# Block scales of the feed-forward tiles: five of their six small operations moved from VectorE to GpSimd

## Chip, cores, metric

One Trainium2 chip, one core of it. The metric is the device time of one execution in microseconds, the median of several runs.

## What is computed

A small vision tower: patches to tokens, an RWKV attention layer, a feed-forward layer with quantized operands, a softmax attention layer, and a mixture of 64 experts. 64 images of 17 tokens make 1088 rows of 256 numbers. The change lies in the feed-forward layer, whose hidden values (1024 for each row) are quantized to a 4-bit format in blocks of 16 before the down projection:

```
def fake_quant_nvfp4(x, global_scale):
    xb = x.reshape(sh[:-1] + (sh[-1] // BLOCK, BLOCK))
    amax = jnp.max(jnp.abs(xb), axis=-1, keepdims=True)
    sc = jnp.clip(amax / FP4_MAX * global_scale, 0.0, FP8_MAX)
    sc8 = sc.astype(jnp.float8_e4m3fn).astype(jnp.float32)
    dq = sc8 / global_scale
    safe_dq = jnp.where(dq == 0.0, 1.0, dq)
    a = jnp.clip(jnp.abs(xb) / safe_dq, 0.0, FP4_MAX)
    q = jnp.sign(xb) * _FP4_VALS[jnp.digitize(a, _FP4_MIDS)]
    return (q * dq).reshape(sh)
gate_out = nvfp4_linear(x, gate_w, s_in[0])
up_out = nvfp4_linear(x, up_w, s_in[0])
hidden = jax.nn.silu(gate_out) * up_out
return nvfp4_linear(hidden, down_w, s_in_down[0])
```

A row has 64 blocks, so a tile of 128 rows has 128 x 64 block scales, and each is made from the block's maximum by a chain of six operations.

## The kernel before

Every engine has its program written out by hand; semaphores are the only order between them. The feed-forward layer goes over 9 tiles of 128 rows (the last has 64). For tile n:

- TensorE makes gate and up products into PSUM (`gate_up`), ScalarE makes silu of the gate (L1312), and VectorE multiplies both into `hid` (L1710).
- VectorE takes the maxima of the 64 blocks into `ham` (L1718), and makes the scales in six small operations on 128 x 64 elements: scaled and clipped maximum `a0` (L1729), its lower bound `low` (L1732), `low` times a power of two plus `a0` (L1738, which rounds to 8 bits), the rounded scale with its sign turned, twice over, in `hsb` (L1744), its product with the inverse of the global scale (L1752), and the reciprocal (L1754). `hss` holds three such rows and there are two of them.
- GpSimd multiplies `hid` by the reciprocals (L623, the division), ScalarE makes its absolute value as 16-bit numbers in `hq` (L1295).
- Two tiles later VectorE rounds it in four large operations of 128 x 1024: L1724, L1735, L1741 (a clamp), and L1749 (times the scale in `hsb`). TensorE transposes `hq`, ScalarE moves it, TensorE makes the down product, and VectorE adds it to `h` (L1468) four tiles after n.

VectorE's loop (L1700 on) has in its pass n the small operations of tile n and the rounding of tile n-2, one in the gaps of the other: while a small operation waits for the one before, a large one is issued. `mark` and `after` count them on one semaphore, `link` is both at once. GpSimd has nothing in this stage but the division, and two memsets before the division of tile 5 (L619, L620), which clear parts of `qT` and `kbd` for the attention. Where the last tile is done, layernorm and attention follow.

Two other places come up below, both in the attention stage: `L644`, GpSimd's four copies of a block of `prT` into `pbd`, each waiting for the one before, and `L1812`, VectorE's subtraction of one SBUF tensor from another (`shared_w` less `shared_h`), twice without a wait between.

Of the kernel before, what the change touches and what calls it, by code (L numbers as in the profile page):

```python
# [15 lines left out]
ALU = mybir.AluOpType  # L16
ACT = mybir.ActivationFunctionType
AX = mybir.AxisListType
# [16 lines left out]
PAIRS = BLK // 2  # L35
E_MAGIC = 2.0 ** 20
Q_MAGIC = 2.0 ** 22
Q_FLOOR = Q_MAGIC * (1.0 + 2.0 ** -7)
# [20 lines left out]
def rows(t):  # L59
    return min(P, N - t * P)  # L60


def bc(ap, axis, n):

    a = ap.unsqueeze(axis)
    shape = list(a.shape)
    shape[axis] = n
    return a.broadcast_to(shape)
# [40 lines left out]
def build(nc, A, out):  # L109
    with ExitStack() as ctx:  # L110
        def sem(name):
            return ctx.enter_context(nc.semaphore(name))
# [24 lines left out]
        gs6 = sb("gs6", [P, 5])  # L137
        gin = sb("gin", [P, 5])
        gil = sb("gil", [P, 5])
# [64 lines left out]
        hid = [reg2.cut([P, I0]) for _ in range(3)]  # L204
        hq = [reg2.cut([P, I0], BF16) for _ in range(4)]
        hqT = [reg2.cut([P, IC, P], BF16) for _ in range(2)]
        ham = [reg2.cut([P, NHB]) for _ in range(2)]
        hss = [reg2.cut([P, 3, NHB]) for _ in range(2)]
        hsm = [reg2.cut([P, NHB], BF16) for _ in range(2)]
        hsb = [reg2.cut([P, 2 * NHB], BF16) for _ in range(3)]  # L210
# [141 lines left out]
        s_xdiv = sem("s_xdiv")  # L352
        s_xabs = sem("s_xabs")
        s_hdiv = sem("s_hdiv")
        s_hinv = sem("s_hinv")
        s_habs = sem("s_habs")
        s_y0 = sem("s_y0")
# [15 lines left out]
        s_hq = sem("s_hq")  # L373
# [193 lines left out]
        def _(pool):  # L567
# [29 lines left out]
            def largest(m):  # L597

                pool.wait_ge(s_wmx, m + 1)
                nc.gpsimd.partition_all_reduce(wmx_all[:, m:m + 1], wmx[:, m:m + 1], P, RMAX).then_inc(s_wmxa, 1)  # L600

            largest(0)
            largest(1)
            nc.gpsimd.memset(upto[:, :], 0.125).then_inc(s_mc, 1)
# [11 lines left out]
            for t in range(NT):  # L616
                if t == 5:
                    pool.wait_ge(s_xqT, 3)
                    nc.gpsimd.memset(qT[:, :, T:SLOT], 0.0).then_inc(s_zero, 1)  # L619
                    nc.gpsimd.memset(kbd, 0.0).then_inc(s_zero, 1)  # L620
                pool.wait_ge(s_hinv, t + 1)
                v = hid[t % 3].rearrange("p (k b r) -> p k b r", k=PAIRS, r=2)
                nc.gpsimd.tensor_tensor(v, v, bc(bc(hss[t % 2][:, 2, :], 1, PAIRS), 3, 2), ALU.mult).then_inc(s_hdiv, 1)  # L623
                if t == NT - 1:
                    ln(2, 0)
# [828 lines left out]
        def _(dve):  # L1454
            chain = [0]

            def link(ins):

                chain[0] += 1
                ins.then_inc(s_dve, 1)  # L1460
                dve.wait_ge(s_dve, chain[0])

            V = nc.vector
# [7 lines left out]
            def mark(ins):  # L1471

                chain[0] += 1
                ins.then_inc(s_dve, 1)
                return chain[0]

            def after(count):
                dve.wait_ge(s_dve, count)
# [94 lines left out]
            def round_weight(m):  # L1573
# [10 lines left out]
                                   op0=ALU.mult, op1=ALU.add).then_inc(s_clsb, 1)  # L1584
# [115 lines left out]
            for n in range(NT + 5):  # L1700
                if n == NT + 3:
                    low_part(0, 0)
                    low_part(1, 1)
                scales, rounding, adding = n < NT, 0 <= n - 2 < NT, 0 <= n - 4 < NT
                if scales:
                    am, (a0, a1, a2) = ham[n % 2], [hss[n % 2][:, i, :] for i in range(3)]
                    low, neg, v, r = hsm[n % 2], hsb[n % 3], hid[n % 3], slice(0, rows(n))
                    dve.wait_ge(s_gate, n + 1)
                    dve.wait_ge(s_gu, 2 * n + 2)
                    V.scalar_tensor_tensor(out=v[r, :], in0=ps[r, 4:6, :].rearrange("p a b -> p (a b)"), scalar=alp[r, 1:2],  # L1710
                                           in1=gate[n % 2][r, :], op0=ALU.mult, op1=ALU.mult).then_inc(s_hid, 1)
                if adding:
                    t = n - 4
                    dve.wait_ge(s_down, t + 1)
                    add_rows(t, 7 if t % 2 else 0, alp[0:rows(t), 2:3], s_h2)
                if scales:
                    dve.wait_ge(s_hid, n + 1)
                    done_s = mark(V.tensor_reduce(am, v.rearrange("p (k b r) -> p b k r", k=PAIRS, r=2), AX.XY, ALU.max,  # L1718
                                                  apply_absolute_value=True))
                if rounding:  # L1720
                    w = n - 2
                    x, q = hid[w % 3], hq[w % 4]
                    dve.wait_ge(s_habs, w + 1)
                    done_r = mark(V.scalar_tensor_tensor(out=x, in0=q, scalar=Q_FLOOR, in1=x, op0=ALU.max, op1=ALU.add))  # L1724
                if scales:
                    after(done_s)
                    if n >= 2:
                        dve.wait_ge(s_hdiv, n - 1)
                    done_s = mark(V.tensor_scalar(a0, am, gs6[:, 4:5], 448.0, ALU.mult, ALU.min))  # L1729
                if scales:  # L1730
                    after(done_s)
                    done_s = mark(V.tensor_scalar(low, a0, 2.0 ** -6, None, ALU.max))  # L1732
                if rounding:
                    after(done_r)
                    done_r = mark(V.scalar_tensor_tensor(out=q, in0=q, scalar=Q_FLOOR, in1=x, op0=ALU.max, op1=ALU.subtract))  # L1735
                if scales:
                    after(done_s)
                    done_s = mark(V.scalar_tensor_tensor(out=a1, in0=low, scalar=E_MAGIC, in1=a0, op0=ALU.mult, op1=ALU.add))  # L1738
                if rounding:
                    after(done_r)  # L1740
                    done_r = mark(V.tensor_scalar(q, q, 6.0, -6.0, ALU.min, ALU.max))  # L1741
                if scales:
                    after(done_s)
                    done_s = mark(V.scalar_tensor_tensor(out=neg.rearrange("p (b r) -> p b r", r=2), in0=bc(low, 2, 2),  # L1744
                                                         scalar=E_MAGIC, in1=bc(a1, 2, 2), op0=ALU.mult, op1=ALU.subtract))
                if rounding:
                    after(done_r)
                    q = q.rearrange("p (k c) -> p k c", k=PAIRS)
                    V.tensor_tensor(q, q, bc(hsb[w % 3], 1, PAIRS), ALU.mult).then_inc(s_hq, 1)  # L1749
                if scales:  # L1750
                    after(done_s)
                    done_s = mark(V.tensor_scalar(a2, neg[:, 0::2], gil[:, 4:5], 1e-24, ALU.mult, ALU.max))  # L1752
                    after(done_s)
                    V.reciprocal(a2, a2).then_inc(s_hinv, 1)  # L1754
                if n - 4 == LN_PARTS[0][1] - 1:
                    ln_variance(2, 0)
                if n - 4 == LN_PARTS[0][1]:
                    ln_finish(2, 0)
# [287 lines left out]
```

## Time and profile before

| | |
|---|---|
| median of 3 runs | 623.29 us (622.12 to 624.65) |
| the profiled execution | 625.0 us, its span 623.3 us |
| VectorE busy | 439.4 us (70%) |
| GpSimd busy | 218.7 us (35%) |
| TensorE busy | 518.0 us (83%) |
| feed-forward tiles, first L1710 to last L1754 | 126.90 to 188.31 us of the span |

The times of single operations, waits and the chain that ended last come from the one profiled execution. An operation's row in the timeline has its start, its duration, the engine and the line, output and inputs by name with their shapes, and in brackets how long the engine had been idle before it and who released it. Nearly all tiles of this stage lie in one large allocation called `region`, so rows are told apart by their lines.

### The profile page before, as it was taken

What the parts mean: (1) busy time and instruction counts of PE and PEld (TensorE: products, weight loads), DVE (VectorE), ACT (ScalarE), POOL (GpSimd) and SP (SyncE); (2) the same over time, 40 slices, a digit from 0 to 9 for tenths busy, and PEclk for the clock granted to TensorE, in tenths of its full rate; (3) what the DMA queues carried; (4) which work ended last, traced back from release to release, by engine and by line L of the source; (5) the groups of instructions that cost most, each with busy time, mean ns of one, the idle gap of its engine ahead of it and who ended that gap; (6) DMA issues with size and microseconds to landing.
All of it is one profiled execution on the core that took longest, in us unless ns stands there. A gap on an engine that the chain in (4) does not pass through costs nothing.

```text
span 623.3 us, 10367 instructions
## 1 busy us (share of the span) xinstructions
PE 518.0 (83%) x3494; PEld 421.2 (68%) x3498; DVE 439.4 (70%) x995; ACT 337.6 (54%) x798; POOL 218.7 (35%) x230
## 2 busy tenths in 40 slices
PE   3986953166555699999999999999999999999875
PEld 2755842023323699999999887876777777777674
DVE  4996998999999546555655713576776777775676
ACT  1577635255444656666666325625666677676600
POOL 2101001022422602222221141237777777777600
PEclk9985987586875699999999999999999999999979
DMA  8980000008200000000000001013777777887492
GB/s 270 381 315 0 1 0 0 0 2 272 79 2 0 1 26 27 26 28 27 26 1 2 2 1 51 22 28 100 200 225 203 230 237 216 230 241 212 143 407 87
DMA packets 43895, 67.33 MB, mean 108 GB/s; under 512 B 11022, under 2 KB 27015, under 8 KB 43716
## 3 DMA queue, kind: packets, MB, share of 16 engines
q1 hardware_dynamic: 36868, 64.62, 32.5%
q0 software_dynamic: 6976, 2.07, 1.7%
q8 instruction: 28, 0.46, 0.3%
q14 instruction: 23, 0.19, 0.1%
HBM read 66.81 MB, written 17.20 MB: 135 GB/s over the span
## 4 chain that ended last, share of the span: by engine, by line
PE 60%; DVE 24%; DMA 5%; ACT 4%; issue 3%; POOL 3%; SPq 0%; DVEq 0%; POOLq 0%; ACTq 0%
PE ps L1089 9%; PE ps L734 6%; PE ps L736 6%; PE ps L735 6%; PE ps L953 5%; PE ps L911 5%; PE ps L786 4%; PE ps L741 4%; DMA region<-x_rows,region 3%; PE ps L943 3%; PE ps L1079 2%; PE ps L925 2%; PE ps L1136 2%; DVE region L1724 2%; PE ps L1097 2%
## 5 line engine op out<-in xcount | busy, mean ns | idle before, releaser
L1089 PE MATMUL ps<-region 128*128 128x352 f32 x256 | 86.4, 460 | 0.3 <-issue 0.3
L1780 DVE TENSOR_TENSOR region<-ps,region 32x136 f32<-32x136 f32 x128 | 38.1, 298 | 55.3 <-PE ps L911 53.8
L685 POOL DMA_INDIRECT region<-x_rows,region x64 | 68.1, 1064 | 20.2 <-issue 15.0
L734 PE MATMUL ps<-nTh,high 128*128 128x272 f32 (+2 forms) x248 | 74.4, 300 | 0.4 <-ACT region L1362 0.4
L735 PE MATMUL ps<-nTl,high 128*128 128x272 f32 (+2 forms) x248 | 71.6, 289 | 0.0
L694 POOL DMA_INDIRECT y_rows<-region x60 | 61.1, 1019 | 21.0 <-issue 14.7
L644 POOL COPY region<-region 32x544 f32<-32x544 f32 x32 | 26.4, 825 | 115.1 <-DVE region L1799 113.6
L1928 DVE SCALAR_TENSOR_TENSOR region<-region,ps 128x176 f32<-128x176 f32 x64 | 25.4, 397 | 42.9 <-ACT region L1439 40.3
L736 PE MATMUL ps<-nTh,pairs_low 128*128 128x272 f32 x192 | 55.6, 290 | 0.0
L1449 ACT ACTIVATE high<-region 88x512 fp32r<-88x512 f32 x64 | 40.3, 630 | 25.4 <-PE ps L736 20.0
L1089 PEld LDWEIGHTS ps<-region 128*128 128x128 f32 x256 | 43.6, 190 | 14.0 <-issue 0.5
L734 PEld LDWEIGHTS ps<-nTh,high 128*128 128x128 f32 (+2 forms) x248 | 46.3, 187 | 2.0 <-ACT region L1362 0.6
L735 PEld LDWEIGHTS ps<-nTl,high 128*128 128x128 f32 (+2 forms) x248 | 46.4, 187 | 0.1
L595 POOL TENSOR_TENSOR rstd<-veps,mhalf 128x6 f32<-128x6 f32 (+1 forms) x8 | 9.2, 1148 | 100.6 <-DVE veps L1487 100.6
L734 PE MATMUL ps<-high,pairs_low 88*128 88x256 f32 x128 | 41.3, 323 | 3.0 <-DVE shared_low L1953 3.0
L623 POOL TENSOR_TENSOR region<-region 128x1024 f32<-128x1024 f32 x9 | 19.2, 2129 | 63.3 <-DVE region L1754 63.3
L741 PE MATMUL ps<-region 128*128 128x256 f32 (+1 forms) x108 | 28.6, 420 | 10.2 <-DMA region<-patches 10.2
L736 PEld LDWEIGHTS ps<-nTh,pairs_low 128*128 128x128 f32 x192 | 36.5, 190 | 0.0
L735 PE MATMUL ps<-w_low,pairs_low 88*128 88x256 f32 x128 | 36.1, 282 | 0.0
L736 PE MATMUL ps<-high,pairs_low 88*128 88x256 f32 x128 | 36.0, 281 | 0.0
L911 PE MATMUL ps<-region 128*128 128x136 f32 x256 | 33.1, 282 | 0.9 <-DVE region L1780 0.9
L953 PE MATMUL ps<-region 128*128 128x256 f32 (+1 forms) x144 | 31.8, 381 | 2.0 <-DVE region L1780 1.5
(264 smaller groups left out, 1353.4 us busy)
## 6 DMA issues: line engine op xcount, KB each, us to landing
region<-moe_w SPq DMA_DIRECT2D x64, 352.0 KB, 3.7
region<-moe_w SPq DMA_DIRECT2D x64, 176.0 KB
y_rows<-zrow SPq DMA_DIRECT2D x1, 6528.0 KB, 25.3
region<-y_rows SPq DMA_DIRECT2D x8, 768.0 KB, 10.5
region<-wqkv SPq DMA_DIRECT2D x8, 384.0 KB, 3.0
region<-ffn_w SPq DMA_DIRECT2D x2, 1024.0 KB, 8.3
region<-patches SPq DMA_DIRECT2D x3, 384.0 KB, 8.3
region<-patches SPq DMA_DIRECT2D x1, 1152.0 KB, 10.7
```

The source lines that it names most:

```text
L644: nc.gpsimd.tensor_copy(pbd[j][r, :, q * T:(q + 1) * T], prT[r, :, 0:T]).then_inc(s_spread, 1)
L685: nc.gpsimd.indirect_dma_start(out=xb[m8], out_offset=None, in_=x_rows, in_offset=bass.IndirectOffsetOnAxis(ap=sloti[:, at:at + 1], axis=0 ...
L694: nc.gpsimd.indirect_dma_start(out=y_rows, out_offset=bass.IndirectOffsetOnAxis(ap=sld[m8], axis=0), in_=yb[m], in_offset=None, bounds_che ...
L734: nc.tensor.matmul(out, parts_a[0], parts_b[0], start=first, stop=False)
L735: nc.tensor.matmul(out, parts_a[0], parts_b[1], start=False, stop=False)
L736: return nc.tensor.matmul(out, parts_a[1], parts_b[0], start=False, stop=last)
L741: nc.tensor.matmul(ps[0:rows(t), t % 8, 0:D], patch[:, c, t * P:t * P + rows(t)], tokw[:, c, :], start=(c == 0), stop=False)
L911: mm = nc.tensor.matmul(ps[:, 4 + g // 2, (g % 2) * 2 * GW:(g % 2 + 1) * 2 * GW], qT[:, 4 * t:4 * t + 4, :].rearrange("p b t -> p (b t)"), ...
L953: mm = nc.tensor.matmul(ps[0:rows(t), 4 + t % 4, 0:D], attnT[:, c, t * P:t * P + rows(t)], wo1[:, c, :], start=(c == 0), stop=(c == HP - 1))
L1089: mm = nc.tensor.matmul(ps[:, 2 + m % 2, 0:2 * EI], xbT[m % 2][:, c, :], w13[m][:, c, :], start=(c == 0), stop=(c == DC - 1))
L1449: nc.scalar.activation(w2_h[m % 2], w2[m], ACT.Copy).then_inc(s_w2h, 1)
L1780: last = V.tensor_tensor(sc[r, s0:s0 + 8, 0:T].rearrange("p (a b) t -> p a b t", a=4), ps[r, 4:8, 0:4 * GW].rearrange("p a (b h t) -> p a ...
```

## The change

The first five of the six small operations go to GpSimd, in front of its division of the same tile, each waiting for the one before on a semaphore of its own (`s_hsc`). VectorE keeps the maxima (which now signal `s_ham`) and the reciprocal, which it issues after the whole rounding of tile n-2. The rounding operations, which had the small ones between them, are linked directly. On GpSimd `low` is made as the lower bound times the power of two in one operation, so that the third and the fourth are plain operations on two tensors; it is kept in 32 bits. Two waits are new for the buffers: the maxima wait for the reciprocal two tiles before, and GpSimd's operation 4 and its division wait for the rounding (`s_hq`).

```diff
+            def tile_scales(t):
+                am, (a0, a1, a2) = ham[t % 2], [hss[t % 2][:, i, :] for i in range(3)]
+                low, neg = a2, hsb[t % 3]
+                pool.wait_ge(s_ham, t + 1)
+                nc.gpsimd.tensor_scalar(a0, am, gs6[:, 4:5], 448.0, ALU.mult, ALU.min).then_inc(s_hsc, 1)
+                pool.wait_ge(s_hsc, 5 * t + 1)
+                nc.gpsimd.tensor_scalar(low, a0, 2.0 ** -6, E_MAGIC, ALU.max, ALU.mult).then_inc(s_hsc, 1)
+                pool.wait_ge(s_hsc, 5 * t + 2)
+                nc.gpsimd.tensor_tensor(a1, low, a0, ALU.add).then_inc(s_hsc, 1)
+                pool.wait_ge(s_hsc, 5 * t + 3)
+                if t >= 3:
+                    pool.wait_ge(s_hq, t - 2)
+                nc.gpsimd.tensor_tensor(neg.rearrange("p (b r) -> p b r", r=2), bc(low, 2, 2), bc(a1, 2, 2),
+                                        ALU.subtract).then_inc(s_hsc, 1)
+                pool.wait_ge(s_hsc, 5 * t + 4)
+                nc.gpsimd.tensor_scalar(a2, neg[:, 0::2], gil[:, 4:5], 1e-24, ALU.mult, ALU.max).then_inc(s_hsc, 1)
+                pool.wait_ge(s_hinv, t + 1)
...
-                pool.wait_ge(s_hinv, t + 1)
+                tile_scales(t)
                 v = hid[t % 3].rearrange("p (k b r) -> p k b r", k=PAIRS, r=2)
+                if t >= 2:
+                    pool.wait_ge(s_hq, t - 1)
...
                 if scales:
                     dve.wait_ge(s_hid, n + 1)
-                    done_s = mark(V.tensor_reduce(am, v.rearrange("p (k b r) -> p b k r", k=PAIRS, r=2), AX.XY, ALU.max,
-                                                  apply_absolute_value=True))
+                    if n >= 2:
+                        dve.wait_ge(s_hinv, n - 1)
+                    V.tensor_reduce(am, v.rearrange("p (k b r) -> p b k r", k=PAIRS, r=2), AX.XY, ALU.max,
+                                    apply_absolute_value=True).then_inc(s_ham, 1)
                 if rounding:
                     w = n - 2
                     x, q = hid[w % 3], hq[w % 4]
                     dve.wait_ge(s_habs, w + 1)
-                    done_r = mark(V.scalar_tensor_tensor(out=x, in0=q, scalar=Q_FLOOR, in1=x, op0=ALU.max, op1=ALU.add))
-                if scales:
-                    after(done_s)
...
+                    link(V.scalar_tensor_tensor(out=x, in0=q, scalar=Q_FLOOR, in1=x, op0=ALU.max, op1=ALU.add))
+                    link(V.scalar_tensor_tensor(out=q, in0=q, scalar=Q_FLOOR, in1=x, op0=ALU.max, op1=ALU.subtract))
+                    link(V.tensor_scalar(q, q, 6.0, -6.0, ALU.min, ALU.max))
                     q = q.rearrange("p (k c) -> p k c", k=PAIRS)
                     V.tensor_tensor(q, q, bc(hsb[w % 3], 1, PAIRS), ALU.mult).then_inc(s_hq, 1)
                 if scales:
-                    after(done_s)
-                    done_s = mark(V.tensor_scalar(a2, neg[:, 0::2], gil[:, 4:5], 1e-24, ALU.mult, ALU.max))
-                    after(done_s)
+                    dve.wait_ge(s_hsc, 5 * n + 5)
                     V.reciprocal(a2, a2).then_inc(s_hinv, 1)
```

On VectorE, pass 2 of the loop in the kernel before, from the first rounding operation of tile 0 to the first operation of tile 3:

```order
L1724 SCALAR_TENSOR_TENSOR region<-region 128x1024 [waits s_habs]
L1729 TENSOR_SCALAR region<-region,gs 128x64 [waits s_hdiv,s_dve]
L1732 TENSOR_SCALAR region<-region 128x64 [waits s_dve]
L1735 SCALAR_TENSOR_TENSOR region<-region 128x1024 [waits s_dve]
L1738 SCALAR_TENSOR_TENSOR region<-region 128x64 [waits s_dve]
L1741 TENSOR_SCALAR region<-region 128x1024 [waits s_dve]
L1744 SCALAR_TENSOR_TENSOR region<-region 128x128 [waits s_dve]
L1749 TENSOR_TENSOR region<-region 128x1024 [waits s_dve]
L1752 TENSOR_SCALAR region<-region,gil 128x64 [waits s_dve]
L1754 RECIPROCAL region<-region 128x64 [waits s_dve]
L1710 SCALAR_TENSOR_TENSOR region<-ps,alp,region 128x1024 [waits s_gu,s_gate]
```

The same place in the changed kernel (its lines: 1743 the maxima, 1749 to 1753 the rounding, 1756 the reciprocal, 1733 the product of gate and up):

```order
L1743 TENSOR_REDUCE region<-region 128x64 [waits s_hinv,s_hid]
L1749 SCALAR_TENSOR_TENSOR region<-region 128x1024 [waits s_habs]
L1750 SCALAR_TENSOR_TENSOR region<-region 128x1024 [waits s_dve]
L1751 TENSOR_SCALAR region<-region 128x1024 [waits s_dve]
L1753 TENSOR_TENSOR region<-region 128x1024 [waits s_dve]
L1756 RECIPROCAL region<-region 128x64 [waits s_hsc]
L1733 SCALAR_TENSOR_TENSOR region<-ps,alp,region 128x1024 [waits s_gu,s_gate]
```

Five operations of 64 or 128 elements are gone from between the large ones, and the reciprocal, last of the pass as before, waits for another engine.

On GpSimd, the whole of this stage in the kernel before:

```order
L623 TENSOR_TENSOR region<-region 128x1024 [waits s_hinv] x5
L619 MEMSET region 128x64x15 [waits s_xqT]
L620 MEMSET region 128x2176
L623 TENSOR_TENSOR region<-region 128x1024 [waits s_hinv] x4
L595 TENSOR_TENSOR rstd<-veps,mhalf 128x6 [waits ln_pow]
```

And in the changed kernel, from the division of tile 4 (L646) over the two memsets (L640, L641) to the division of tile 5:

```order
L646 TENSOR_TENSOR region<-region 128x1024 [waits s_hq,s_hinv]
L640 MEMSET region 128x64x15 [waits s_xqT]
L641 MEMSET region 128x2176
L609 TENSOR_SCALAR region<-region,gs 128x64 [waits s_ham]
L611 TENSOR_SCALAR region<-region 128x64 [waits s_hsc]
L613 TENSOR_TENSOR region<-region 128x64 [waits s_hsc]
L617 TENSOR_TENSOR region<-region 128x128 [waits s_hq,s_hsc]
L620 TENSOR_SCALAR region<-region,gil 128x64 [waits s_hsc]
L646 TENSOR_TENSOR region<-region 128x1024 [waits s_hq,s_hinv]
```

Each tile has five more operations on GpSimd; those of tile 5 stand behind the two memsets.

## Rows read from the trace of the kernel before

**Rows 1.** The page: span, and the chain that ended last by engine.

```profile
span 623.3 us, 10367 instructions
...
PE 60%; DVE 24%; DMA 5%; ACT 4%; issue 3%; POOL 3%; SPq 0%; DVEq 0%; POOLq 0%; ACTq 0%
```

**Rows 2.** Waits of VectorE, 126.9 to 188.2 us: in total, times, longest.

```profile
DVE region L1710 <- ACT region L1312: 0.7, 1, 0.7
```

**Rows 3.** Timeline of VectorE, tile 6 (start us, us, engine, line).

```profile
166.28 1.18 DVE L1710 SCALAR_TENSOR_TENSOR region<-ps,alp,region 128x1024 f32<-128x1024 f32 x1
...
167.78 1.21 DVE L1718 TENSOR_REDUCE region<-region 128x64 f32<-128x1024 f32 x1
168.91 1.22 DVE L1724 SCALAR_TENSOR_TENSOR region<-region 128x1024 f32<-128x1024 bf16 x1
170.05 0.25 DVE L1729 TENSOR_SCALAR region<-region,gs 128x64 f32<-128x64 f32 x1
...
170.44 1.22 DVE L1735 SCALAR_TENSOR_TENSOR region<-region 128x1024 bf16<-128x1024 bf16 x1
...
171.71 0.42 DVE L1741 TENSOR_SCALAR region<-region 128x1024 bf16<-128x1024 bf16 x1
...
172.25 0.68 DVE L1749 TENSOR_TENSOR region<-region 128x1024 bf16<-128x1024 bf16 x1
172.85 0.25 DVE L1752 TENSOR_SCALAR region<-region,gil 128x64 f32<-128x64 bf16 x1
173.13 0.55 DVE L1754 RECIPROCAL region<-region 128x64 f32<-128x64 f32 x1
173.60 1.19 DVE L1710 SCALAR_TENSOR_TENSOR region<-ps,alp,region 128x1024 f32<-128x1024 f32 x1
```

**Rows 4.** Tile 0: timeline of VectorE, then the chain that ended last.

```profile
128.21 1.22 DVE L1718 TENSOR_REDUCE region<-region 128x64 f32<-128x1024 f32 x1
...
130.86 0.55 DVE L1754 RECIPROCAL region<-region 128x64 f32<-128x64 f32 x1
...
131.49 2.14 POOL region L623
...
135.41 1.01 ACT region L1312
```

**Rows 5.** Timeline of VectorE and GpSimd, around 161 and 188 us.

```profile
161.02 1.91 POOL L620 MEMSET region<- 128x2176 f32 x1
161.71 1.27 DVE L1729 TENSOR_SCALAR region<-region,gs 128x64 f32<-128x64 f32 x1
...
188.39 2.12 POOL L623 TENSOR_TENSOR region<-region 128x1024 f32<-128x1024 f32 x1 [5.18 <-DVE region L1754]
...
188.54 3.06 DVE L1724 SCALAR_TENSOR_TENSOR region<-region 128x1024 f32<-128x1024 bf16 x1
```

**Rows 6.** Timeline, GpSimd's copies with and without VectorE's subtractions, then their durations.

```profile
338.72 2.80 POOL L644 COPY region<-region 32x544 f32<-32x544 f32 x4 [13.53 <-DVE region L1799]
...
355.66 0.89 DVE L1812 TENSOR_TENSOR shared_low<-region,high 128x704 fp32r<-128x704 f32 x1
355.75 1.32 POOL L644 COPY region<-region 32x544 f32<-32x544 f32 x1 [14.22 <-DVE region L1799]
356.46 1.34 DVE L1812 TENSOR_TENSOR shared_low<-region,high 128x704 fp32r<-128x704 f32 x1
357.13 1.18 POOL L644 COPY region<-region 32x544 f32<-32x544 f32 x1
...
L644 POOL COPY region<-region x32: 636/662/1392, 236.8 to 359.1; 32x544 f32<-32x544 f32 x32
```

**Rows 7.** Small GpSimd operations: by form (busy, mean ns), one line (ns min/median/max).

```profile
L595 POOL TENSOR_TENSOR rstd<-veps,mhalf 128x3 f32<-128x3 f32 x4 | 3.4, 854 | 28.8 <-DVE veps L1487 28.8
L584 POOL CAST ident_bf<-ident 128x128 bf16<-128x128 f32 x1 | 0.3, 290 | 0.1
...
L666 POOL TENSOR_TENSOR region<-region x12: 761/772/1620, 389.2 to 425.9; 128x272 f32<-128x272 f32 x8, 96x272 f32<-96x272 f32 x4
```

More of the change, by code:

```diff
@@ L354, in build @@
         s_hdiv = sem("s_hdiv")
+        s_ham = sem("s_ham")
+        s_hsc = sem("s_hsc")
         s_hinv = sem("s_hinv")
@@ L1705, in _ @@
                 if scales:
-                    am, (a0, a1, a2) = ham[n % 2], [hss[n % 2][:, i, :] for i in range(3)]
-                    low, neg, v, r = hsm[n % 2], hsb[n % 3], hid[n % 3], slice(0, rows(n))
+                    am, a2 = ham[n % 2], hss[n % 2][:, 2, :]
+                    v, r = hid[n % 3], slice(0, rows(n))
                     dve.wait_ge(s_gate, n + 1)
@@ L1723, in _ @@
                     dve.wait_ge(s_habs, w + 1)
-                    done_r = mark(V.scalar_tensor_tensor(out=x, in0=q, scalar=Q_FLOOR, in1=x, op0=ALU.max, op1=ALU.add))
-                if scales:
-                    after(done_s)
[L1727 to L1730, printed above, removed]
-                    after(done_s)
[L1732 to L1736, printed above, removed]
-                    after(done_s)
[L1738 to L1747, printed above, removed]
+                    link(V.scalar_tensor_tensor(out=x, in0=q, scalar=Q_FLOOR, in1=x, op0=ALU.max, op1=ALU.add))
+                    link(V.scalar_tensor_tensor(out=q, in0=q, scalar=Q_FLOOR, in1=x, op0=ALU.max, op1=ALU.subtract))
+                    link(V.tensor_scalar(q, q, 6.0, -6.0, ALU.min, ALU.max))
                     q = q.rearrange("p (k c) -> p k c", k=PAIRS)
@@ L1750, in _ @@
                 if scales:
-                    after(done_s)
-                    done_s = mark(V.tensor_scalar(a2, neg[:, 0::2], gil[:, 4:5], 1e-24, ALU.mult, ALU.max))
-                    after(done_s)
+                    dve.wait_ge(s_hsc, 5 * n + 5)
                     V.reciprocal(a2, a2).then_inc(s_hinv, 1)
```

## The prediction

> **What bounds the kernel now.** The page first: the span of the profiled execution is 623.3 us, TensorE holds 60% of the chain that ended last and VectorE 24% [rows 1]. So a few us of VectorE count only where VectorE itself sets the pace, and the question is whether it does so in the feed-forward tiles. The waits of VectorE between 126.9 and 188.2 us answer it: one wait in 61 us, of 0.7 us [rows 2]. The timeline of one tile (number 6) shows the same from inside: from one L1710 at 166.28 to the next at 173.60 the engine goes without a gap, 7.32 us for a tile [rows 3]. What VectorE gains or loses here per tile, the next stage (layernorm, then attention, each waiting for the last tile) gets one for one.
>
> Where do the six small operations lie? Take the end of the reduction L1718 as zero: 167.78 + 1.21 = 168.99 [rows 3]. L1724 (rounding of tile n-2) ends at 1.14; then small and large operations alternate, and while a small one waits for its predecessor a large one runs. L1724 to L1749 take 172.25 - 168.91 = 3.34 us to start, L1749 to L1752 0.60, to L1754 0.28, to the next L1710 0.47: that L1710 starts at 4.61. In tile 0, which has no rounding, the five bare small operations cost 130.86 - (128.21 + 1.22) = 1.43 us [rows 4].
>
> **What VectorE saves.** Five operations go from it. A dependent operation starts 0.03 us after the one before has ended (172.85 + 0.25 = 173.10, next at 173.13 [rows 3]). So the four rounding operations alone, now linked one to another, would end at 1.14, then 1.14 + 0.03 + 1.22 = 2.39, then 2.39 + 0.03 + 0.42 = 2.84, then 2.84 + 0.03 + 0.68 = 3.55. With nothing in their way the reciprocal would follow L1749 by 0.60 (start to start), and the next L1710 would start at 2.87 + 0.60 + 0.47 = 3.94: a saving of 0.67 us per tile. Not the 1.2 us that the five durations add up to, since they already lay between and over the large ones.
>
> **What stands in the way: the two engines hold one another up.** Three places of the trace show it. First, L1724 at 188.54 takes 3.06 us in place of its 1.22 (as in [rows 3]), while GpSimd's division runs from 188.39 to 190.51 [rows 5]. Second, L1729 takes 1.27 us in place of 0.25, and ends 0.05 us after the memset of 161.02 + 1.91 = 162.93 [rows 5]. Third, and this is the pattern that the change makes, GpSimd's copies beside VectorE's subtractions [rows 6]: a copy takes 0.64 to 0.66 us, but 1.32 and 1.18 beside them, and it ends 0.52 and 0.51 us after the end of the subtraction it met (357.07 against 356.55; 358.31 against 357.80). The second subtraction, 0.89 us alone, takes 1.34 and ends 357.80 - 357.07 = 0.73 us after the copy. So: they take turns; a GpSimd operation that waited ends its own duration less 0.12 after the VectorE operation; the VectorE operation that waited for it ends its own duration less 0.15 after it. Those that met are operations with two tensors in SBUF, as L1724, L1735 and L1749 are, or a tensor with a scalar (L1729), as L1741 is. An L1710 beside the division, which has one tensor in PSUM, keeps its 1.2 us (173.60 [rows 3]; the division starts 0.08 us after the reciprocal of 173.13 ends), and the division is over before the next rounding starts: that is why it has cost nothing in tiles 0 to 7. The five moved operations start when the reduction ends, which is just when the rounding starts: they meet all four.
>
> The Trainium skill says this too: "SBUF — State Buffer", section "Who interferes with whom", has VectorE and GpSimd sharing a pair of ports under an exclusive lock held for a whole instruction, for VectorE operations with two SBUF inputs against GpSimd reads. Taken to the letter, whole durations would add, which comes to about the second rival's time below in place of the forecast's. The trace agrees that they take turns, and its 0.12 and 0.15 us say that the start-up of an instruction is hidden.
>
> **What the five cost on GpSimd.** None of them is in the trace. Nearest rows [rows 7]: a one-input cast of 128 elements 0.29 us; two-input operations of 272 elements 0.77 us and of 1024 elements (the division [rows 5]) 2.12 us, so 1.80 ns per element and 0.28 fixed, which makes 0.40 us for 64 elements and 0.51 for 128. The dearest small one is the power of 3 elements, 0.85 us. For the three tensor_scalar I take 0.30 us (half the elements of the cast, but two functions and for two of them a scalar from memory); the bounds are 0.2 and 0.85. From one to the next 0.07 us: four linked copies of 0.64 to 0.66 us with no subtraction beside them take 2.80 us [rows 6], so (2.80 - 0.66) / 3 = 0.71 from start to start. Into the chain 0.08 (a division at 131.49 after a reciprocal that ends at 130.86 + 0.55 = 131.41 [rows 4]); out of it I take 0.04, close to VectorE's own 0.03.
>
> **A tile with rounding, step by step.** Operation 1 ends at 1.14 - 0.12 + 0.30 = 1.32. L1735 ends at 2.39 (its own chain, not later for GpSimd: 1.32 - 0.15 + 1.22 = 2.39). Operation 2: 2.57. The clamp: 2.84 (2.57 - 0.15 + 0.42). Operation 3: 2.84 - 0.12 + 0.40 = 3.12. The multiply: 3.12 - 0.15 + 0.68 = 3.65. Operation 4: 3.65 - 0.12 + 0.51 = 4.04. Operation 5, with VectorE idle: 4.04 + 0.07 + 0.30 = 4.41. Reciprocal at 4.45, next L1710 at 4.92. Against 4.61 that is **+0.31 us a tile**: VectorE is given back 0.67, and loses it, and more, in the wait for operations 4 and 5. Behind that reciprocal stand L1710 of the next tile and, for it, TensorE's next gate and up products; and GpSimd's division.
>
> **The others.** Tile 0: 0.08 + 3 x 0.30 + 0.40 + 0.51 + 4 x 0.07 + 0.04 = 2.21 in place of 1.43, +0.78. The division of tile 0 is on the chain to tile 2 (division, then ScalarE, L1312, L1710 [rows 4]), so the +0.78 goes through, and the 0.7 us that VectorE waited there hides nearly all of the second +0.78, of tile 1: together +0.8. Tiles 2, 3, 4, 6, 7, 8: 6 x 0.31 = +1.9. Tile 5: GpSimd clears qT and kbd first, until 162.93. L1729 starts 170.05 - 168.99 = 1.06 after the reduction in tile 6, so the reduction of tile 5 ended at 161.71 - 1.06 = 160.65, 2.28 before the clearing was over. Until now the clearing blocked L1729 for 1.27 - 0.25 = 1.02 us, which put the next L1710 at 4.61 + 1.02 = 5.63; now it delays operation 1, which gets in after L1735 (2.39 - 0.12 + 0.30 = 2.57). The second follows the clamp (3.02), the multiply ends at 3.55, the third at 3.83, then 4.41 and 4.78, L1710 at 5.29: -0.3. The added waits for hq and hinv have their releaser one operation or a whole tile earlier and cost nothing. After tile 8 nothing is changed, the block of 3.06 - 1.22 = 1.84 us at 188.54 stays. Sum: 0.8 + 1.9 - 0.3 = **+2.4 us**. The profiled execution took 625.0 us (span 623.3), the median of the runs is 623.3; a difference is the same on either: 627.4 by the former, **625.7** by the median, which I give.
>
> **The rivals.**
> *Dearer operations on GpSimd* (slower). With 0.45 us for a tensor_scalar, by the same steps, L1710 comes at 5.37, +0.76 a tile; tiles 0 and 1 together +1.7, tile 5 +0.1; in all +6.4: 629.7. With 0.85 it would be +17. For it: the power of 3 elements costs 0.85 and almost nothing in that is elements. Against: the cast of 128. The difference to "no change" is passed at about 0.33 us for each.
> *No turns between linked operations* (slower). If GpSimd gets in only once the rounding is over, or every operation adds in full, the chain of 1.97 us stands behind 3.55: L1710 at 6.03, +1.42 a tile; 0.8 + 6 x 1.42 + 0.4 = +9.7: 633. For it: nothing in the trace has small GpSimd operations against linked VectorE ones. Against: a copy got in between two subtractions that were issued without any gap at all [rows 6].
> *The small operations are not held up* (faster). If reads of 64 elements slip past VectorE's, the chain of 2 us lies under 3.55 us of rounding and each tile saves its 0.67: 0.8 - 6 x 0.67 - 0.65 = -3.9: 619.4. It decides from the point at which operation 5 ends before L1749 does. Against: the copies, whose own reads are not long either, waited to the end.
> *The change doesn't do what it says*: the order of instructions shows five operations on GpSimd for each tile and one left on VectorE, so this has no chance of its own.
>
> **Chances.** A measurement of this kernel tells 0.5% (3.1 us) from nothing. Forecast (between 622 and 626.4): 0.46. Dearer operations: 0.28. No turns: 0.12. Not held up: 0.14. So faster 0.14, same 0.46, slower 0.40. The range leaves out the fastest case and the far end of the dearest operations: 621 to 634.
>
> **What the profile after would show.** Right: five GpSimd rows a tile, each ending 0.2 to 0.4 us after a rounding operation of VectorE; that line of rounding still at its 1.2 us (no 3 us); a wait of VectorE for GpSimd of 0.7 to 0.9 us in each tile; 7.6 us from L1710 to L1710; L1729's 1.27 us gone. Wrong: tensor_scalar on GpSimd over 0.4 us, the first GpSimd operation starting only after the multiply, or a tile of 6.7 us. Layernorm, attention and experts should keep their lengths; if they don't, the sum was made of the wrong stage.

## The result: 3.5 us slower, and the profile after

| | before | changed |
|---|---|---|
| median, 6 runs each | 623.34 us (622.12 to 624.65) | 626.82 us (626.45 to 630.09) |
| ratio | | 1.0062, 95% interval 1.0038 to 1.0086 |
| profiled execution, its span | 625.0, 623.3 us | 630.09, 628.4 us |

Slower by 0.6%, inside the range (621.0 to 634.0), 1.1 us above the forecast of 625.7. It is above the band of the forecast itself (622 to 626.4, chance 0.46): 3.5 us is more than the 3.1 us that I had called nothing, so the outcome is the one that had the chance 0.40, slower. The page of the changed kernel, span and busy times:

```profile
span 628.4 us, 10380 instructions
...
PE 523.0 (83%) x3494; PEld 422.0 (67%) x3498; DVE 430.8 (69%) x950; ACT 337.9 (54%) x798; POOL 252.4 (40%) x275
```

VectorE is busy for 8.6 us less than before, GpSimd for 33.7 us more, and the kernel is longer. The waits of VectorE in the tiles answer to [rows 2]:

```profile
DVE region L1756 <- POOL region L620: 15.2, 9, 2.7
```

Where there was one wait of 0.7 us there are nine for GpSimd's last operation, 15.2 us in total. Tile 6 in the timeline answers to [rows 3] (L1733 the product, L1743 the maxima, L1749 to L1753 the rounding, L1756 the reciprocal; on GpSimd L609 to L620 the five operations):

```profile
169.46 1.18 DVE L1733 SCALAR_TENSOR_TENSOR region<-ps,alp,region 128x1024 f32<-128x1024 f32 x1
...
170.96 1.21 DVE L1743 TENSOR_REDUCE region<-region 128x64 f32<-128x1024 f32 x1
...
172.09 1.21 DVE L1749 SCALAR_TENSOR_TENSOR region<-region 128x1024 f32<-128x1024 bf16 x1
172.28 1.40 POOL L609 TENSOR_SCALAR region<-region,gs 128x64 f32<-128x64 f32 x1 [0.52 <-DVE region L1743]
...
173.34 1.22 DVE L1750 SCALAR_TENSOR_TENSOR region<-region 128x1024 bf16<-128x1024 bf16 x1
173.77 1.35 POOL L611 TENSOR_SCALAR region<-region 128x64 f32<-128x64 f32 x1
174.60 0.43 DVE L1751 TENSOR_SCALAR region<-region 128x1024 bf16<-128x1024 bf16 x1
175.06 0.69 DVE L1753 TENSOR_TENSOR region<-region 128x1024 bf16<-128x1024 bf16 x1
175.20 0.73 POOL L613 TENSOR_TENSOR region<-region 128x64 f32<-128x64 f32 x1
...
176.01 0.43 POOL L617 TENSOR_TENSOR region<-region 128x128 bf16<-128x128 f32 x1
...
176.53 0.51 POOL L620 TENSOR_SCALAR region<-region,gil 128x64 f32<-128x64 bf16 x1
177.07 0.55 DVE L1756 RECIPROCAL region<-region 128x64 f32<-128x64 f32 x1 [1.32 <-POOL region L620]
177.54 1.19 DVE L1733 SCALAR_TENSOR_TENSOR region<-ps,alp,region 128x1024 f32<-128x1024 f32 x1
```

The tile takes 177.54 - 169.46 = 8.08 us in place of 7.32. The rounding runs through at its usual durations (1.21, 1.22, 0.43 and 0.69 us), as if it were alone; GpSimd's first three operations are stretched, and the last two stand behind the multiply, where VectorE waits 1.32 us. Tile 0 has no rounding and shows the bare prices:

```profile
128.49 0.52 POOL L609 TENSOR_SCALAR region<-region,gs 128x64 f32<-128x64 f32 x1 [24.15 <-DVE region L1743]
129.10 0.45 POOL L611 TENSOR_SCALAR region<-region 128x64 f32<-128x64 f32 x1
129.63 0.32 POOL L613 TENSOR_TENSOR region<-region 128x64 f32<-128x64 f32 x1
130.03 0.43 POOL L617 TENSOR_TENSOR region<-region 128x128 bf16<-128x128 f32 x1
130.56 0.51 POOL L620 TENSOR_SCALAR region<-region,gil 128x64 f32<-128x64 bf16 x1
131.10 0.55 DVE L1756 RECIPROCAL region<-region 128x64 f32<-128x64 f32 x1 [2.72 <-POOL region L620]
```

From the first L1733 (125.85) to the rounding behind the last reciprocal (194.02) the stage takes 68.2 us; before it was 188.54 - 126.90 = 61.6. That is +6.5 us, and two things are then to be explained: why a tile costs +0.76 and not +0.31, and why 6.5 us in the stage make 3.5 us in the median.

### The profile page after: what moved, and what is told of

Read it like the earlier page. It is cut to its first block, busy times and chain, and to the rows that moved or that the text cites. A ratio compares the mean times of both kernels' runs of the same rounds, so it can differ in the third digit from the quotient of the medians.

```text
span 628.4 us, 10380 instructions
## 1 busy us (share of the span) xinstructions
PE 523.0 (83%) x3494; PEld 422.0 (67%) x3498; DVE 430.8 (69%) x950; ACT 337.9 (54%) x798; POOL 252.4 (40%) x275
## 4 chain that ended last, share of the span: by engine, by line
PE 56%; DVE 22%; POOL 8%; DMA 5%; issue 4%; ACT 3%; SPq 0%; DVEq 0%; POOLq 0%; ACTq 0%
PE ps L1112 9%; PE ps L757 6%; PE ps L759 6%; PE ps L758 6%; PE ps L976 5%; PE ps L934 5%; DMA region<-x_rows,region 4%; PE ps L764 3%; PE ps L966 3%; PE ps L1102 2%; PE ps L948 2%; PE ps L1159 2%; POOL region L609 2%; POOL region L611 2%; DVE region L1733 2%
## 5 line engine op out<-in xcount | busy, mean ns | idle before, releaser
L667 POOL COPY region<-region 32x544 f32<-32x544 f32 x32 | 26.4, 826 | 114.9 <-DVE region L1801 113.5
L1195 ACT ACTIVATE xn<-h,mom 128x256 f32<-128x256 f32 (+1 forms) x36 | 17.9, 498 | 27.8 <-DVE h L1491 27.8
```

Source lines behind the costliest of these rows:

```text
L667: nc.gpsimd.tensor_copy(pbd[j][r, :, q * T:(q + 1) * T], prT[r, :, 0:T]).then_inc(s_spread, 1)
```

## The experiments

My theory: the operations are dearer on GpSimd than I took them, and the first ones are held up by the rounding. The rivals are that the new order on VectorE is what costs (e2, e4), or that GpSimd is slow for a reason of its own (e4). For the total, either a later stage gives something back, or the comparison itself moves (e1, e6, e9 to e12).

Each kernel was compared with the kernel before on its own chip. Chips differ: on that of e1 to e4, and on that of e11 and e12, the kernel before takes 655 us, because the experts' part is longer there (in e1 249 us from 411.1 on, in the first profiles 217), while the tiles have the same lengths. A tile is from one product to the next in the profile, tile 6 or 7.

| run | median, before there | ratio (95% interval) | a tile |
|---|---|---|---|
| e1 changed kernel again | 663.2, 655.6 | 1.0121 (1.0087 to 1.0154) | 8.1 |
| e2 order only, all on VectorE | 660.1, 655.6 | 1.0059 (1.0031 to 1.0088) | 8.20 |
| e3 operations 4 and 5 back | 658.9, 655.6 | 1.0051 (1.0022 to 1.0080) | 7.59 |
| e4 rounding without two inputs | 652.0, 655.6 | 0.9930 (0.9904 to 0.9956) | 6.66 |
| e5 addition in the wait | 629.7, 622.7 | 1.0114 (1.0067 to 1.0160) | 8.08, 8.19 |
| e6 before, late clearing | 620.2, 622.7 | 0.9977 (0.9948 to 1.0006) | 7.3 |
| e7 e6 with split clearing | 619.7, 622.7 | 0.9959 (0.9932 to 0.9986) | 7.3 |
| e8 chain held back | 637.5, 622.7 | 1.0260 (1.0203 to 1.0317) | 9.52 |
| e9 before again | 623.1, 623.6 | 1.0004 (0.9974 to 1.0034) | 7.3 |
| e10 changed kernel, third | 626.6, 623.6 | 1.0057 (1.0030 to 1.0083) | 8.1 |
| e11 changed, late clearing | 660.6, 654.6 | 1.0094 (1.0065 to 1.0122) | 8.1 |
| e12 before, late clearing | 655.4, 654.6 | 1.0012 (0.9988 to 1.0036) | 7.3 |

**e2: the order alone.** From the kernel before (the diff is abridged, as are those of e3, e4 and e5):

```diff
+ link(maxima); rounding: link, link, link, multiply
+ link(V.tensor_scalar(a0, am, gs6[:, 4:5], 448.0, ALU.mult, ALU.min))
+ link(V.tensor_scalar(low, a0, 2.0 ** -6, None, ALU.max))
+ ... the other three and the reciprocal, linked, behind the rounding on VectorE
- the same operations between those of the rounding
```

> All six small operations back on VectorE, but in the changed kernel's order: after the whole rounding, linked one to another. My theory: each small operation then costs its bare time, so a tile takes 6.65 - 0.60 + 0.71 + 1.43 = about 8.2 us, as dear as the changed kernel's 8.09, and the run is 3 to 4 us slower than the kernel before. The rival, that only GpSimd's slowness matters and the order is harmless, expects no change against the kernel before (7.3 us a tile).

A tile takes 8.20 us (167.96 to 176.16), 8.2 expected, and the run is 4.5 us slower than the kernel before, 3 to 4 expected. So the changed kernel's order costs on VectorE alone what the changed kernel costs: moving five operations to another engine has bought back 0.1 us of it. The interleaving of the kernel before was worth 0.9 us a tile.

**e3: operations 4 and 5 on VectorE.** From the changed kernel:

```diff
- nc.gpsimd.tensor_tensor(neg..., ALU.subtract); nc.gpsimd.tensor_scalar(a2, neg[:, 0::2], ...)
+ dve.wait_ge(s_hsc, 3 * n + 3)
+ link(V.tensor_tensor(neg.rearrange(...), bc(a2, 2, 2), bc(a1, 2, 2), ALU.subtract))
+ link(V.tensor_scalar(a2, neg[:, 0::2], gil[:, 4:5], 1e-24, ALU.mult, ALU.max))
```

> Operations 1 to 3 stay on GpSimd, 4 and 5 go to VectorE behind the rounding. If only what stands behind the multiply costs anything, and 1 to 3 lie under the rounding though each is held up there, the wait of 1.32 us before the reciprocal becomes one for operation 3 of about 0.2 us and 0.57 us of VectorE work: 7.6 us a tile, half a us less than the changed kernel, +0.3 against before, so 2 to 3 us back of the loss. If the held-up operations 1 and 2 were the cost by themselves, a tile stays at 8.1.

Timeline of e3, the step behind the multiply:

```profile
172.99 0.73 POOL L613 TENSOR_TENSOR region<-region 128x64 f32<-128x64 f32 x1
173.75 0.29 DVE L1750 TENSOR_TENSOR region<-region 128x128 bf16<-128x128 f32 x1 [0.21 <-POOL region L613]
```

The wait is 0.21 us, a tile 7.59, both as expected: what stands behind the multiply is what costs. The median is 4.3 us below that of e1, where 2 to 3 were expected.

**e4: the same chain beside a rounding that doesn't meet it.** It leaves the first two rounding steps out and puts two reductions in their place:

```diff
- link(V.scalar_tensor_tensor(out=x, in0=q, scalar=Q_FLOOR, in1=x, ...)); link(... out=q ...)
+ for _ in range(2):
+     link(V.tensor_reduce(hsm[w % 2], x.rearrange("p (k b r) -> p b k r", ...), AX.XY, ALU.max, ...))
```

> The changed kernel, with the first two rounding operations replaced by two reductions of the same 1024 elements (1.22 us each, one SBUF input). It leaves the rounding of the hidden values out; the clamp and the multiply stay. If GpSimd's first two operations last 1.40 and 1.35 us because two-input operations of VectorE hold them up, they fall to 0.52 and 0.45 here, the whole chain of 2.6 us is nearly done when the multiply is, the wait before the reciprocal goes, and a tile takes 6.7 us: some 10 us less than the changed kernel over the tiles with rounding. If they are slow for another reason (semaphores, a busy sequencer), a tile stays at 8.1.

Timeline of e4, VectorE and GpSimd:

```profile
168.90 2.46 DVE L1750 TENSOR_REDUCE region<-region 128x64 bf16<-128x1024 f32 x2
169.09 0.51 POOL L609 TENSOR_SCALAR region<-region,gs 128x64 f32<-128x64 f32 x1 [0.52 <-DVE region L1743]
169.68 0.44 POOL L611 TENSOR_SCALAR region<-region 128x64 f32<-128x64 f32 x1
170.20 0.32 POOL L613 TENSOR_TENSOR region<-region 128x64 f32<-128x64 f32 x1
170.60 0.43 POOL L617 TENSOR_TENSOR region<-region 128x128 bf16<-128x128 f32 x1
171.13 0.79 POOL L620 TENSOR_SCALAR region<-region,gil 128x64 f32<-128x64 bf16 x1
171.40 0.43 DVE L1752 TENSOR_SCALAR region<-region 128x1024 bf16<-128x1024 bf16 x1
```

Beside work of the same length with one input, operations 1 and 2 take 0.51 and 0.44 us and not 1.40 and 1.35; all five fit under the rounding, no wait is left, and a tile takes 6.66 us; the median is 11.2 us below that of e1, some 10 expected. This settles the mechanism: with such a rounding the change would have gained 0.66 us a tile, and the meeting with two-input operations turns that into a loss of 0.76. VectorE's order is the same as in the changed kernel, so it isn't the order by itself either. One more thing shows here: the clamp, which reads one tensor, holds GpSimd up too. Operation 5 starts beside a reduction and then meets the clamp (from 171.40); it takes 0.79 us in place of 0.51 and ends at 171.92, 0.09 after the clamp (171.83).

**e8: no overlap at all.** From the changed kernel:

```diff
 pool.wait_ge(s_ham, t + 1)
+if t >= 2:
+    pool.wait_ge(s_hq, t - 1)
```

> The changed kernel, with GpSimd's chain made to wait for the multiply of the rounding, so that none of it overlaps. The bare chain is 2.6 us; now 1.3 us of it lies behind the multiply. If taking turns hides operations 1 to 3 as I read the trace, a tile becomes 1.3 us longer, +9 us against the changed kernel (about 636). If overlap gives nothing because the operations are only stretched by what they overlap, it stays at 627.

Timeline of e8: the chain starts behind the multiply, at its bare prices, and VectorE waits 2.76 us.

```profile
171.79 0.51 POOL L611 TENSOR_SCALAR region<-region,gs 128x64 f32<-128x64 f32 x1 [1.48 <-DVE region L1755]
...
174.37 0.55 DVE L1758 RECIPROCAL region<-region 128x64 f32<-128x64 f32 x1 [2.76 <-POOL region L622]
```

A tile is 9.52, 1.44 us longer than the changed kernel's 8.08 (1.3 expected), so the overlap does hide operations 1 to 3.

**e5: filling the wait.** From the changed kernel; its expectation failed:

```diff
-if adding: ... add_rows(t, ...)          (ahead of the maxima)
+if adding: ... add_rows(t, ...)          (behind the multiply, ahead of the reciprocal)
```

> The changed kernel with the addition of tile n-4 (0.48 us, one input in PSUM) moved from ahead of the maxima into VectorE's wait before the reciprocal. If that wait of 1.32 us is idle time and the chain through it sets the pace, each of the five tiles with an addition loses 0.40 us: -2 us against the changed kernel. If TensorE or ScalarE had slack-less work behind the addition, nothing is gained.

Timeline of e5, VectorE and ScalarE:

```profile
175.12 0.48 DVE L1491 SCALAR_TENSOR_TENSOR h<-ps,alp,h 128x256 f32<-128x256 f32 x1
...
175.64 0.51 ACT L1195 ACTIVATE xn<-h,mom 128x256 f32<-128x256 f32 x1 [3.06 <-DVE h L1491]
...
176.15 1.09 ACT L1335 ACTIVATE region<-ps,alp 128x1024 f32<-128x1024 f32 x1
...
177.27 1.28 DVE L1733 SCALAR_TENSOR_TENSOR region<-ps,alp,region 128x1024 f32<-128x1024 f32 x1 [0.19 <-ACT region L1335]
```

The wait shrinks from 1.32 to 0.93 us, and nothing is won: ScalarE's squares (L1195) wait for the addition, 3.06 us here, the silu of the next tile (L1335) stands behind them, and the next product now waits for it. This tile takes 8.08 us, as in the changed kernel, and the next 8.19. The addition had no slack after all.

**e1, e9, e10: how far the comparison moves.** Unaltered kernels.

> The changed kernel once more, unaltered. In its first profile the tile stage (first product of gate and up to the first rounding after the last reciprocal) was 6.6 us longer than before, but the medians differ by only 3.5 us. If the stage really costs 6.6 us and something downstream gives some back, this profile shows the stage at the same length and a span near 625 with a later stage shorter; if the first profile was only a slow sample, the stage is again 8.09 us a tile and the difference lies in stages that the change doesn't touch.

> The kernel before, unaltered, measured as if it were a change. The tile stage of the changed kernel is 6.6 us longer in both of its profiles, but the two comparisons gave +3.5 and +7.6 us. This run shows how far a comparison moves with no change at all: I expect a ratio of 1.000 with an interval of about 0.4% to either side, which would make 3.5 and 7.6 two readings of the same 6.6.

> The changed kernel a third time, beside the one above on the same chip. If the stage's 6.6 us arrive in full at the end, the ratio is 1.0105 (+6.5 us). If some later stage regularly gives part of it back, it is 1.006 again, and the profile shows a later stage that is shorter than in the run above.

The kernel before against itself gives 1.0004, with 0.3% to either side; the changed kernel gives +3.5, +7.6 and +3.0 us (medians 626.6 and 623.6). The stage is the same in each of its profiles (first to last product 59.8 us in the first, in e1 and in e10). But one row is not: it lasts 4.58 us in both profiles of the kernel before and in two of the three of the changed one, and 0.87 in e10. GpSimd's late clearing beside VectorE's last layernorm steps, first the first profile of the changed kernel, then e10:

```profile
209.09 0.90 POOL L652 MEMSET region<- 128x960 f32 x1
209.17 0.16 DVE L1516 TENSOR_TENSOR nwt<-rstd 128x3 f32<-128x3 f32 x1 [0.97 <-POOL rstd L597]
209.37 0.17 DVE L1517 TENSOR_TENSOR nwt<-nwt,veps 128x3 f32<-128x3 f32 x1
209.57 4.58 DVE L1518 TENSOR_SCALAR nwt<-nwt 128x3 f32<-128x3 f32 x1
...
210.37 3.76 POOL L655 MEMSET region<- 128x2176 f32 x2
```

```profile
208.80 0.90 POOL L652 MEMSET region<- 128x960 f32 x1
...
209.28 0.87 DVE L1518 TENSOR_SCALAR nwt<-nwt 128x3 f32<-128x3 f32 x1
...
209.63 0.50 POOL L653 MEMSET region<- 128x480 f32 x1
```

A tensor_scalar of three numbers for each partition starts 0.48 us after the first of four memsets in both. In one execution it ends 0.02 us after the fourth (214.15 against 214.13), in the other 0.02 us after the second (210.15 against 210.13). The runs of e10 fall into two heaps, five at 623.8 to 624.8 and seven at 626.2 to 629.4; those of the kernel before on that chip into seven at 618.6 to 620.1 and sixteen at 621.5 to 625.4. e10's profile, with the short row, is one of the low heap (623.83); the first profile, with the long one, is the highest of its six runs (630.09, the others 626.45 to 627.36). Heap against heap the changed kernel is about 4 us slower (medians 624.1 against 620.0, 627.9 against 623.7).

**e6, e7, e11, e12: the clearing held back.** One line, in the kernel before (e6, e7, e12) and in the changed one (e11):

```diff
 pool.wait_ge(s_down, NT)
+pool.wait_ge(ln_scale, 6)
 nc.gpsimd.memset(vT[:, :, T:SLOT], 0.0)
```

and in e7 also kbd in two halves before the divisions of tiles 6 and 7.

> The kernel before, with one wait added: GpSimd's clearing of vT, sc and pbd (5 us in four memsets) waits until VectorE has made the shift of the last layernorm part. In the trace of before one tensor_scalar of 3 elements (L1495) takes 4.58 us and ends with the last memset. If memsets without a gap hold VectorE's scalar operations out until the last one, this takes about 4 us off the kernel before (619). If that row is only a badly recorded semaphore, or the attention stage waits for the cleared buffers, nothing or less than 1 us.

> As e6, and the clearing of kbd (1.91 us at once before the division of tile 5) is cut in two halves of 0.95 us before the divisions of tiles 6 and 7, where they end before VectorE's first scalar operation. Expected: L1729's 1.27 us in tile 5 is gone, 1 us less than e6. If it isn't the memset that blocks it, the same as e6.

> The changed kernel with GpSimd's late clearing held back until the layernorm's shift is made (the edit of e6). The runs so far fall in two heaps 3 to 4 us apart for either kernel, and the profiles differ in one row: the tensor_scalar of 3 elements (L1495, now L1518) takes 4.58 us or 0.87. With the clearing held back that chance is gone. Against e12 on the same chip: +6.5 us if the tile stage's cost arrives whole; about +4 if TensorE's clock, which in the changed kernel's profiles rises earlier in the attention stage, gives 2 us back as a rule. Its runs should form one heap, within 3 us.

> e6 once more, as the partner of e11 on the same chip: one heap of runs about 3 us below the median of the kernel before, its profile with L1495's successor at 0.17 us.

Timeline of e6, where the same operation takes 0.17 us and the clearing starts behind it, and of e7, tile 5, where L1729's successor is down from 1.27 to 0.25:

```profile
202.74 0.17 DVE L1496 TENSOR_SCALAR nwt<-nwt 128x3 f32<-128x3 f32 x1
...
203.43 0.90 POOL L630 MEMSET region<- 128x960 f32 x1 [1.12 <-DVE shift L1498]
```

```profile
160.87 0.25 DVE L1734 TENSOR_SCALAR region<-region,gs 128x64 f32<-128x64 f32 x1
```

Both rows are as expected. The medians gain less: 2.5 us for e6, where 4 were expected (its interval reaches over 1), and 3.0 for e7, whose interval (0.9932 to 0.9986) leaves out 1. Two things make the difference. First, the row is 4.4 us shorter, but from the first product of the tiles to the first `nTl` (VectorE's first write for the attention's projections) e6 takes 79.1 us and the kernel before 82.1, 3.0 less, since that write now waits 1.33 us for ScalarE. Second, on the chip of e6 the kernel before falls into heaps as well, nine runs at 618.5 to 620.3 and fourteen at 622.3 to 625.3. Ten of e6's twelve runs lie at 617.9 to 620.9 and all twelve of e7's at 616.5 to 620.9: beside the lower heap nothing is gained, the upper one is gone. That is what the short row should do, and it speaks for this row as what makes the heaps, though runs without a profile don't show it.

On the chips where the kernel takes 655 us no heaps can be told apart, and there e12 missed its expectation: no gain (655.4 against 654.6), and runs from 650.1 to 662.7. With the clearing held back in both, the changed kernel costs 660.6 - 655.4 = 5.3 us, and e11's runs lie within 2.6 us but for two. That doesn't decide between the 6.5 and the 4 of its expectation.

## Why the prediction was right, and where it was wrong

**Right: what holds up what.** The stage was the right one, nothing was won from VectorE's freed 0.67 us a tile, and the loss sits in the wait for operations 4 and 5. e4 shows the cause: take two of the three two-input operations away and the change gains. The Trainium skill's rule ("SBUF — State Buffer", section "Who interferes with whom") that a VectorE operation with two SBUF inputs contends with a GpSimd operation that reads SBUF, and a reduction doesn't, agrees with e4's 0.51 against 1.40 us.

Of the signs of being wrong that I had named one came true, a tensor_scalar on GpSimd over 0.4 us. Of the signs of being right, the rounding keeps its 1.2 us and L1729's 1.27 us is gone, but the wait is 1.32 us and not 0.7 to 0.9, and the tile 8.08 and not 7.6.

**Wrong in size: the price of a tensor_scalar on GpSimd.** I took 0.30 us; it is 0.44 to 0.52. The two tensor_tensor came out below my line, 0.32 and 0.43 for 0.40 and 0.51. A one-input cast was a bad neighbour: a tensor_scalar with two functions is the dearer form here, though it reads one tensor. From the end of the maxima (172.17 in tile 6), predicted and measured:

| end of | predicted | measured |
|---|---|---|
| operation 1 | 1.32 | 1.51 |
| L1750 | 2.39 | 2.39 |
| operation 2 | 2.57 | 2.95 |
| clamp | 2.84 | 2.86 |
| operation 3 | 3.12 | 3.76 |
| multiply | 3.65 | 3.58 |
| operation 4 | 4.04 | 4.27 |
| operation 5 | 4.41 | 4.87 |
| next product starts | 4.92 | 5.37 |

**Wrong in the path: operation 3's turn.** In my sum operation 2 ends before the clamp and operation 3 before the multiply. Measured, operation 2 ends 0.09 us after the clamp, when the multiply has already started, and operation 3 comes after the multiply. The price of operation 2 doesn't do that alone: by the rule of my sum it would end at 2.39 - 0.12 + 0.45 = 2.72, before the clamp's 2.86. The clamp held it, by the same 0.09 us after its end as it held operation 5 in e4. An estimate from these rows says what that turn is worth: with my own prices but operation 3 behind the multiply, operation 3 ends at 3.58 - 0.12 + 0.40 = 3.86, operation 4 at 3.86 + 0.07 + 0.51 = 4.44, operation 5 at 4.44 + 0.07 + 0.30 = 4.81, and the next product starts at 4.81 + 0.04 + 0.47 = 5.32. So the lost turn makes most of the 0.45 us between 4.92 and 5.37. The dearer operation 5 (0.21) is nearly made up for by the cheaper operations 3 and 4 (0.08 each).

**Wrong in part: "the VectorE operation that waited for it".** The 0.15 us step from the copies [rows 6] made the multiply (L1753) late in my sum. It wasn't: L1749 to L1753 keep 1.21, 1.22, 0.43 and 0.69 us. L1750 starts at 173.34 while operation 1 runs on until 173.68, and still takes its 1.22. Only GpSimd is held up; why a read of 64 elements doesn't hold VectorE while the copies of 544 do is not shown.

**The stage is a rival's, not the forecast's.** *Dearer operations*, worked out at 0.45 us, had +0.76 a tile, +1.7 for tiles 0 and 1, +0.1 for tile 5, +6.4 in all. Measured: +0.68 in tile 2, then +0.76 to +0.78; tiles 0 and 1 (137.15 - 125.85) - (136.45 - 126.90) = +1.75; tile 5 (169.46 - 160.85) - (166.28 - 157.94) = +0.27; in all +6.5. That this rival meets 5.37 to the hundredth is luck. Its steps have GpSimd hold the rounding up, so that the multiply ends at 3.95 and operation 3 keeps its turn; the multiply ends at 3.58 and the turn is lost, and the two errors cancel. *No turns* is refuted by e8, *not held up* by the 1.40 and 1.35 us of operations 1 and 2, which e4 brings back to 0.51 and 0.44.

**The total: near by luck, and only partly settled.** The stage lost 6.5 us where I had 2.4; my median came out near because part of the 6.5 us doesn't show in the comparison. In the first profile it does: 6.5 less 1.05 us, by which the tiles started earlier (125.85 against 126.90; over all profiles the start lies between 125.1 and 127.0), less 0.4 us in the attention and the experts, makes the 5.1 us between the spans. In the medians the chance of L1518 is in the way, which I hadn't counted because I had not asked what that 4.58 us row was. With it removed 5.3 us are left, within the error of 6.5 (1.0094 less 1.0012, each 0.3% uncertain). That the other five runs of the first comparison had the short row fits their times, but only the profiled ones show it.

Another part lies in TensorE's granted clock, which has two levels here, 0.50 (1.2 GHz) and 1.00 (2.4 GHz). In each of the three profiles of the changed kernel it reaches 1.00 before the projections begin or within their first two us (in the first profile and e1 it falls back to 0.50 between); in the two of the kernel before it stays at 0.50 for their first 5 and 7 us. From the first `nTl` to the first transpose of the scores these take 26.2, 26.2 and 25.0 us in the changed kernel, 26.4 and 27.4 in the kernel before. So 0.2 to 2.4 us of the stage's loss come back there. What TensorE did before doesn't tell the cases apart. In the 9 us before the first `nTl` it was busy for 6.0 us in e10 and in e11, and for 4.4 in the two first profiles and in e1 and e9. Yet in the first pair e11 (`nTl` at 210.71) starts the projections low and e10 (211.18) doesn't, and of the four the two of the kernel before start low and the other two don't. Stretches of TensorE in e10, then in e11: length, busy time, instructions, granted clock, DMA share, GB/s:

```profile
208.00:211.00 3.00, 2.16 (x10) 0.50 0.00 0
211.00:214.00 3.00, 2.17 (x14) 0.84 0.00 0
214.00:217.00 3.00, 3.00 (x26) 1.00 0.02 5
```

```profile
210.00:213.00 3.00, 2.17 (x10) 0.50 0.00 0
213.00:216.00 3.00, 3.00 (x14) 0.50 0.03 5
216.00:219.00 3.00, 3.00 (x19) 0.67 0.00 0
```

Of all the other profiles, e2 to e8, e11 and e12, none has the early rise. Whether the changed kernel meets it as a rule, and what sets it off, stays open.

## What to carry to other kernels

Small operations between large ones cost little where they are, because a dependent one starts while an independent large one runs: ask for the uncovered time (0.67 us a tile here) and not for the sum of durations (1.2). Before moving work to GpSimd look at what VectorE does in that very stretch: beside reductions (e4) and operations with an input in PSUM (in e5 operation 4 beside the addition keeps its 0.43 us) it is free. Beside operations with two SBUF inputs, and beside the clamp, a step ends only after the large operation has ended. A step whose turn comes a little late loses a whole large operation, so a sum of alternating steps is only as good as its tightest gap: here operation 2 ended 0.06 us after the multiply had started. And a row of a few numbers that takes microseconds is worth a question, since the spread of all measurements may hang on it.

## What the hardware showed that I had not expected

- On GpSimd a tensor_scalar of 128 x 64 takes 0.44 to 0.45 us with constants and 0.50 to 0.52 with a scalar from memory; a tensor_tensor of the same size takes 0.32, of 128 x 128 elements 0.43.
- Small GpSimd operations that read don't hold VectorE's two-input operations up (1.22 us with and without), while copies of 544 elements do (0.89 to 1.34 us [rows 6]).
- A clamp on VectorE (one 16-bit tensor, constants) holds a GpSimd operation up as well. In e4, behind a reduction, operation 5 meets only the clamp where it should have ended, takes 0.79 us in place of 0.51 and ends 0.09 us after the clamp; operation 2 of the changed kernel ends 0.09 us after the clamp too, 0.23 later than L1750 alone would have made it (2.95 against 2.72).
- Memsets in a row can keep a scalar operation of VectorE out until the end of the fourth, 4.58 us, or only until the end of the second, 0.87 us, in the same program and with the same start against the first. Operations with two inputs (L1516, L1517) pass beside the same memset at 0.16 and 0.17 us.
- With the same busy time of TensorE before it, the granted clock rose at the start of the projections in e10 and 7 us later in e11.
